# First layer of a graph network: edges sorted by source bucket on the chip and gathered, in place of scatter-adds to DRAM

## The reference

```python
# layer 0: both edge arrays are used with the first row as target
w0_features = x @ w0
w1_features = x @ w1
dst, src = (edge_index[0], edge_index[1])      # edge_index = [src, dst]: the target is the array src
neighbours = segment_sum(w1_features[src], dst, num_segments=N)
x = layernorm(x + relu(w0_features + neighbours))
# layer 1: 8 edge types, 8 heads of 32: GAT with a table per type
h_all = einsum('nf,rof->rno', x, W)
scores = leaky_relu(h_src . attn_src + h_dst . attn_dst)       # per edge and head
w = softmax of scores over the edges of each dst
x = layernorm(x + segment_sum(h_src * w, dst))
```

## Time and profile before

| | us |
|---|---|
| median of 3 runs | 3920.17 (3910.32 to 3921.48) |
| the profiled execution | 3891.99 |
| its span, first to last instruction | 3890.1 |
| POOL busy | 2379.8 (61%) |
| PE busy | 2260.3 (58%) |
| DVE busy | 1898.7 (49%) |
| ACT busy | 1099.7 (28%) |

### The profile page before, as it was taken

One profiled execution on the slowest core, in us unless ns is written; L12 is line 12 of the kernel. 1 busy time (PEld: TensorE's weight loads), 2 busy tenths in 40 slices (PEclk: granted clock), 3 DMA queues, 4 the chain that ended last, 5 costly groups with the idle time before them and its releaser, 6 DMA issues.

```text
span 3890.1 us, 43658 instructions
## 1 busy us (share of the span) xinstructions
PE 2260.3 (58%) x8426; PEld 1550.0 (40%) x8427; DVE 1898.7 (49%) x6684; ACT 1099.7 (28%) x2537; POOL 2379.8 (61%) x1848
## 2 busy tenths in 40 slices
PE   5444444444444444444999926777776676777660
PEld 4333333333333333332555514555545444555440
DVE  2433333333333333332333315777776676777677
ACT  2211222122212221221333303344444333444330
POOL 0477888888888888885111065666666665666601
PEclk8766676666666766676999957888888887888875
DMA  9678876777776767677656433333333333333303
GB/s 339 137 99 136 150 88 88 88 88 88 88 89 88 88 87 88 88 88 165 222 217 227 174 110 82 94 92 98 94 93 93 95 93 89 96 96 96 93 23 114
DMA packets 318535, 443.64 MB, mean 114 GB/s; under 512 B 49188, under 2 KB 273642, under 8 KB 311504
## 3 DMA queue, kind: packets, MB, share of 16 engines
q0 software_dynamic: 169520, 236.24, 38.2%
q1 hardware_dynamic: 141696, 152.01, 13.4%
q10 hardware_dynamic: 7200, 54.07, 3.4%
HBM read 216.80 MB, written 218.81 MB: 112 GB/s over the span
## 4 chain that ended last, share of the span: by engine, by line
issue 31%; PE 29%; DMA 19%; DVE 9%; ACT 5%; POOL 4%; DVEq 1%; another core or an unknown queue 1%; POOLq 0%; ACTq 0%; SPq 0%; PEldq 0%
PE ps L1370 12%; DMA sums_d<-edge_z,idx_slot 11%; PE ps L1315 9%; DMA sums_d<-sums,idx_slot 7%; POOL sums_d L985 4%; PE ps L1361 3%; DVE nodes L636 3%; DVE region L624 2%; ACT edge_z L1083 2%; DVE region L614 1%; PE ps L1223 1%; ACT sums L1083 1%; PE ps L1295 1%; ACT region L1159 1%; DVE region L619 1%
## 5 line engine op out<-in xcount | busy, mean ns | idle before, releaser
L1025 POOL DMA_INDIRECT region<-ha_d,idx_t x880 | 920.5, 1046 | 567.6 <-issue 329.3
L1266 PE MATMUL ps<-region,edge_z 128*128 x1760 | 649.6, 533 | 653.6 <-ACT edge_z L1091 642.4
L1370 PE MATMUL ps<-region 128*128 128x264 f32 x1760 | 681.8, 533 | 375.2 <-DVE nodes L636 236.3
L985 POOL DMA_INDIRECT sums_d<-sums,idx_slot x440 | 689.3, 1567 | 240.6 <-issue 109.6
L985 POOL DMA_INDIRECT sums_d<-edge_z,idx_slot x440 | 686.4, 1560 | 143.9 <-issue 120.1
L1266 PEld LDWEIGHTS ps<-region,edge_z 128*128 128x128 f32 x1760 | 455.2, 272 | 774.9 <-issue 688.4
L1370 PEld LDWEIGHTS ps<-region 128*128 128x128 f32 x1760 | 385.4, 248 | 604.4 <-issue 381.3
L439 DVE TENSOR_TENSOR idx_slot<-dup,edge_z 128x4 int32<-128x4 f32 x220 | 35.9, 163 | 968.8 <-DMA sums_d<-edge_z,idx_slot 512.8
L636 DVE TENSOR_TENSOR nodes<-ps,nodes 128x264 f32 x880 | 378.7, 430 | 141.3 <-DVE nodes L636 68.2
L1315 PE MATMUL ps<-region,edge_z 128*128 128x512 f32 x800 | 351.6, 593 | 0.0
L1361 PEld LDWEIGHTS ps<-edge_z,region 128*128 128x128 f32 x1760 | 276.7, 229 | 80.1 <-issue 62.2
(11 more groups left out here) (173 smaller groups left out, 2567.5 us busy)
## 6 DMA issues: line engine op xcount, KB each, us to landing
ha_d<-region ACTq DMA_DIRECT2D x50, 1056.0 KB, 4.0
row<-step_rows_d SPq DMA_DIRECT2D x220, 128.0 KB
sums_d<-sums SPq DMA_DIRECT2D x4, 6400.0 KB, 28.8
region<-sums_d SPq DMA_DIRECT2D x100, 256.0 KB, 3.7
region<-ha_d,idx_t POOLq DMA_INDIRECT x880
edge_z<-level_d SPq DMA_DIRECT2D x55, 136.0 KB
kl_d<-nodes SPq DMA_DIRECT2D x8, 903.0 KB
edge_z<-kl_d SPq DMA_DIRECT2D x55, 129.0 KB
```

The lines of the kernel that those rows point to most:

```text
L985: g.indirect_dma_start(sums_d[u], bass.IndirectOffsetOnAxis(ap=idx_slot[:, 0, 4 * q + u:4 * q + u + 1], axis=0), sums[h][:, u, :], None, b ...
L1025: g.indirect_dma_start(rows[s][:, k, :], None, ha_rows, bass.IndirectOffsetOnAxis(ap=idx_t[:, B * b + k:B * b + k + 1], axis=0), bounds_ch ...
L1266: mm = t.matmul(ps[:, 2 + 2 * h + u // 2, (u % 2) * D:(u % 2) * D + D], lhsT=counts[h][:, u, :], rhs=y_sb[:, ds(tile[4 * q + u] * D, D)], ...
L1370: t.matmul(ps[:, u, 0:AW], lhsT=sel[q][:, u, :], rhs=rows[s][:, 4 * q + u, :], start=True, stop=True).then_inc(segs, 1)
```

## The change

The scatter loop, `sums_d`, `step_rows_d` and the search for equal sources go. In their place:

1. **Sort.** Edges lie as [128, 896] (row p, column e). The bucket of an edge is `src >> 8`, 25 buckets (BK) of 256 nodes. 13 masks are made on DVE and 12 on ACT, each with its count; TensorE sums the counts over partitions; DVE works out at which column of 128 cells each bucket starts. Then, for each of the 25 buckets, DVE runs a scan over a mask and multiplies it with the bucket's own edges (`put`), and POOL adds the result to `q_row` (128 x 896). The cell numbers are turned by TensorE, and 30 batches (NBT) of 28 columns (TB) move the values to their cells: DVE makes one-hots of 64 places (28 x 64) and three times in four those of 105 windows (28 x 105), ACT the fourth; POOL multiplies the places with the values; TensorE multiplies both (28 matmuls, 64 columns wide) and, after a copy by DVE, by another one-hot of 856 columns from ACT (two matmuls, 428 wide).
2. **Products.** Meanwhile TensorE computes x @ [w1, w0] tile by tile from xT loaded in chunks; y goes to DRAM (`y_d`), x @ w0 to SBUF (`sums0`) as the start of the sums.
3. **Gathered sums.** 856 columns of 128 cells (COLS) in 214 groups of four (NG): POOL gathers 128 rows of `y_d`, ACT makes a one-hot over 256 nodes, TensorE multiplies (two matmuls of 256 columns for each column), DVE adds 128 x 512 into `sums0`. The preparation of the second layer's steps is set between these groups.
4. **Node stage** without `first_product` and without parts: DVE takes the larger of zero and `sums0`, and adds x.

```diff
+            for t in range(BK):
+                if t >= 2:
+                    v.wait_ge(places, t - 1)
+                v.tensor_tensor_scan(count[t % 2], ones[:, 0:1].to_broadcast([P, KR]), masks[t], start[:, t:t + 1],
+                                     ALU.mult, ALU.add).then_inc(scans, 1)
+                if t >= 1:
+                    put(t - 1)
...
+            for t in range(1, BK):
+                g.wait_ge(places, t + 1)
+                g.wait_ge(summed, t)
+                g.tensor_tensor(q_row, q_row, place[t % 3], ALU.add).then_inc(summed, 1)
...
+            for k in range(NBT):
+                places_of(k)
+                if k + 1 < NBT and not on_scalar(k + 1):
+                    windows_of(k + 1)
+                if k:
+                    halves_of(k - 1)
...
+            for k in range(NBT):
+                g.wait_ge(at_made, k + 1)
+                g.tensor_tensor(at[k % 3], at[k % 3], v_col[:, TB * k:TB * k + TB].unsqueeze(2).to_broadcast([P, TB, HC]),
+                                ALU.mult).then_inc(at_filled, 1)
...
+            def move(k):
+                t.wait_ge(at_filled, k + 1)
+                window_ready(t, k)
...
+                for j in range(TB):
+                    mm = t.matmul(ps[0:WW, 2 + k % 2, 0:HC], lhsT=win[k % 4][:, j, :], rhs=at[k % 3][:, j, :],
+                                  start=(j == 0), stop=(j == TB - 1))
+                mm.then_inc(moved, 1)
+            def settle(k):
+                t.wait_ge(halves_made, k + 1)
+                t.wait_ge(s_made, k + 1)
+                for h in range(2):
+                    mm = t.matmul(ps[:, 4 + h, 0:OH], lhsT=halves[k % 2][0:WW, :, :].rearrange("p s n -> p (s n)"),
+                                  rhs=S_c[k % 2][0:WW, h * OH:(h + 1) * OH], start=(k == 0), stop=(k == NBT - 1))
+                mm.then_inc(o_ps, 1)
...
+            def gather_columns(c):
+                if c >= RING:
+                    g.wait_ge(segs0, 4 * (c - RING) + 4)
+                g.sem_inc(pool_turns, 1)
+                for u in range(4):
+                    k = 4 * c + u
+                    g.indirect_dma_start(rows0[c % RING][:, u, :], None, y_d,
+                                         bass.IndirectOffsetOnAxis(ap=y_idx[:, k:k + 1], axis=0),
+                                         bounds_check=node_bound, oob_is_err=True).then_inc(gath[c % 4][c % RING // 4], 16)
...
+            def sum_columns(c):
+                t.wait_ge(gath[c % 4][c % RING // 4], 64 * (c // RING + 1))
+                t.wait_ge(sel0_made, c + 1)
+                for u in range(4):
+                    if c:
+                        t.wait_ge(added0, 4 * (c - 1) + u + 1)
+                    for h in range(2):
+                        mm = t.matmul(ps[:, u, h * D:(h + 1) * D], lhsT=sel0[c % 4][:, u, h * P:(h + 1) * P],
+                                      rhs=rows0[c % RING][:, u, :], start=True, stop=True)
+                    mm.then_inc(segs0, 1)
...
-            def scatter(it):
-                for q in range(4):
-                    h = q % 2
-                    g.wait_ge(sums_copied, 4 * it + q + 3)
-                    g.wait_ge(slots_ready, 4 * it + q + 1)
-                    for u in range(4):
...
-                        g.indirect_dma_start(sums_d[u],
-                                             bass.IndirectOffsetOnAxis(ap=idx_slot[:, 0, 4 * q + u:4 * q + u + 1], axis=0),
-                                             sums[h][:, u, :], None, bounds_check=node_bound, oob_is_err=True,
-                                             compute_op=ALU.add).then_inc(scattered[h][u], 16)
```

More of the change, by code:

```diff
@@ L317, in in_batches, with on_scalar, window_ready @@
                 body(i, i % 4, i // 4)
+        def on_scalar(k):
+            return k % 4 == 0
+        def window_ready(eng, k):
+            if on_scalar(k):
+                eng.wait_ge(win_a, k // 4 + 1)
+            else:
+                eng.wait_ge(win_v, k - k // 4)
+        AT = {"pads": 2, "rows": 12, "firsts": 16, "tiles": 20, "gather": 34, "local": 46, "turn": 50, "edges": 68,
+              "square": 76, "borders": 92, "whole": 108, "links": 124}
         @block.vector
         def _(v):
-            n = [0]
             n = [0]
@@ new lines, in _ @@
+            do(v.tensor_scalar(count[0], bt, float(BK), None, ALU.is_lt))
+            v.scalar_tensor_tensor(out=v_row, in0=v_row, scalar=1.0, in1=count[0], op0=ALU.add,
+                                   op1=ALU.mult).then_inc(v_made, 1)
+            v.wait_ge(v_made, 1)
+            v.wait_ge(sort_ps, PS["counts"])
+            before_p, first_p, past_p, total_p = [ps[:, 7, BK * k:BK * (k + 1)] for k in range(4)]
+            each = ones[:, 0:1].to_broadcast([P, BK])
+            do(v.tensor_scalar(cols_i, total_p, float(P - 1), None, ALU.add))
@@ new lines, in _ @@
+            for g in range(NG):
+                if g % 4 == 0:
+                    some = min(16, COLS - 4 * g)
+                    v.load(bucket_regs[0:some], bucket_row[0:1, 4 * g:4 * g + some])
+                    bucket = [v.snap(r, min_val=0, max_val=BK - 1) for r in bucket_regs[0:some]]
+                add_columns(g, bucket[4 * (g % 4):4 * (g % 4) + 4])
+                if g == AT["pads"]:
+                    pad_rows()
+                if g == AT["rows"]:
+                    edge_rows()
+                if g == AT["tiles"]:
+                    step_tiles()
+                if AT["tiles"] < g <= AT["tiles"] + BLK:
+                    step_tiles_of(g - AT["tiles"] - 1)
+                if g == AT["local"]:
+                    step_places()
+                if AT["turn"] < g <= AT["turn"] + 2 * BLK and (g - AT["turn"]) % 2 == 0:
+                    turned_places((g - AT["turn"]) // 2 - 1)
+                if g == AT["edges"]:
+                    edge_features()
+                if g == AT["square"]:
+                    square_digits()
+                if g == AT["borders"]:
+                    borders()
+                if g == AT["whole"]:
+                    whole_steps()
+                if g == AT["links"]:
+                    link_rows()
+                    SU["end"] = n[0]
@@ L1002, in inverse_deviation @@
+            g.wait_ge(y_ready, 1)
+            for c in range(NG):
+                if 4 * c <= OH < 4 * c + 4:
+                    g.wait_ge(y_ready, 2)
+                gather_columns(c)
+                if c == AT["gather"]:
+                    gather_step_rows()
             def inverse_deviation(it, par):
@@ new lines, in keep_products @@
+            def keep_products(tile):
+                par, h = tile // 2 % 2, tile % 2
+                a.wait_ge(y_ps, tile + 1)
+                if tile >= 4 and h == 0:
+                    a.wait_ge(y_stored[par], 16 * ((tile // 2 - 2) // 2 + 1))
+                a.copy(y_two[par][:, h, :], ps[:, tile % 2, 0:D]).then_inc(y_kept, 1)
+                a.copy(sums0[:, tile * D:(tile + 1) * D], ps[:, tile % 2, D:2 * D]).then_inc(y_done, 1)
+            for tile in range(NT):
+                keep_products(tile)
```

946 lines of the change are left out of this document (510 added, 436 removed).

## The result

The changed kernel takes 3808.57 us (median of 4 runs, 3789.35 to 3825.79), the kernel before 3915.24 in the same comparison (4 runs, 3883.64 to 3921.48): a ratio of 0.9752, 95% interval 0.9714 to 0.9791, so 2.5% faster. I had forecast 3825 us and 2.4%. The profiled execution took 3815.19 us with a span of 3813.4.

The account below looks back on a forecast made before the run. Bound: a 1672 us scatter stage paced by POOL's indirect DMAs. Steps of 45, 130, 18, 414, 1154 and 398 us start the second layer at 2163 instead of 2258 us; own time 3797 plus 28 gives 3825 us, range 3665 to 3910.

Parts of the forecast that it names:

- Step 1: Start to the counts: edges and bucket numbers by 15 us, then masks and small operations; 45 us.
- Step 2: Bucket loop: VectorE's scan and multiply and GpSimd's add exclude each other, 5.1 us a bucket; 130 us.
- Step 4: The 30 batches of moves: TensorE mostly at 1.2 GHz, 13.8 us a batch; 414 us.
- rival (a): Moves: TensorE gets 2.4 GHz, VectorE with GpSimd sets 9.0 us a batch; 144 us less, 3681 us; chance 0.22.
- Step 5: Gather stage: GpSimd's issue paces it, 1.33 us a gather, 5.3 us a group, the rest fits under; 1154 us.
- theory C: Gather stage, from the experiments' expectations: TensorE's clock sets the stage; separate semaphores would bring no change.
- rival (c): Gather stage: TensorE stays at 1.2 GHz, 7.5 us a group, 1605 us, total 4282 us; chance 0.10.
- Step 6: Node stage: 10 us to the first table, then 25 pairs at 15.05 us; 398 us.
- the 28 us I added: Total: the earlier kernel's profiled execution was 28 us below its runs' median, so 28 us were added to 3797.

Follow-up runs that it names:

- early_masks: Changed kernel with VectorE making the masks before the small tensors that wait for attention loads, and 17 masks in place of 13; 3791.88 us, ratio 0.972.
- no_fill: Changed kernel without GpSimd's multiply in the moves, so all gathered rows are wrong or row 0; 4018.7 us, ratio 1.028, moves 214 us.
- together: Changed kernel with 17 VectorE masks, VectorE's own fill, and eight banks with one news increment per four columns from column 288; 3748.57 us, ratio 0.9605.
- one_gather: Changed kernel with three of the four gathers of each group left out; 3363.44 us, ratio 0.8645, gather stage 847 us.
- no_adds: Changed kernel without VectorE's first-layer adds and TensorE's wait for them; 3756.94 us, ratio 0.9656, gather stage 1240 us.

## Why the prediction was right, and where it was not

**Step 1, to the counts, was 17 us short.** The arithmetic of the masks held (2.1 us each, twelve in 25 us), but not their start: I had let VectorE have the bucket numbers at 15 us, with 28 as the far bound. It had them at 28.8, after waiting for the attention loads until 25.0; the edges landed no earlier, as early_masks shows. Two small readings were off as well: the two prices that I took from the earlier trace rows give 1.0 ns for each further element, not 0.83 (a pass over 896 took 1.04 us, forecast 0.95, with less wait between), and the 64 short passes, which the earlier trace rows price at 0.20 us and I at 0.17, took 13.8 us in place of 11, hidden behind the masks.

**Step 2, the bucket loop, held**: 124.4 us for 25, 5.0 each. The scan takes 2.03 us (forecast 1.9), the multiply 1.06, GpSimd's add 2.07. The exclusion I read from the earlier trace rows is plainer here, in two pieces in order of time of the changed kernel:

```profile
90.48 4.00 DVE L462 TENSOR_TENSOR_SCAN region<-ones,region 128x896 f32<-128x896 f32 x1
90.52 2.07 POOL L1087 TENSOR_TENSOR region<-region 128x896 f32<-128x896 f32 x1 [2.94 <-DVE region L456]
```

The scan's record begins 0.04 us ahead of the add's, but it took 4.00 us, while the first two scans, beside which GpSimd did nothing, took 4.06 together. So the scan did its work after the add. The Trainium skill (SBUF — State Buffer, section "SBUF: two separate sides") says that two such instructions exclude each other for the whole of one, and by that rule the trace agrees.

**Step 4, the moves, failed by its share of half clock.** I had put 13.8 us a batch, nine of ten at 1.2 GHz, and it was 8.4 on average, most at 2.4 GHz. The prices at either level were nearly right and a little high: 12.8 us at half clock (forecast 14.3), and with the exclusion 6.7 to 8.1 (forecast 9.0). The fast level itself was a little better than I had it: 6.6 us a batch for TensorE alone (forecast 7.9). I had reasoned from the earlier trace rows that so few dense columns would leave TensorE slow, and had read there that the clock, once it fell among the 16-column passes, stayed at 0.50. It did not stay. In the kernel before it was low for 10.2 us, and this line of the same view follows:

```profile
98.00:118.00 20.00, 13.76 (x56) 1.00 0.95 361
```

In no_fill, where it never waits, it was at full clock from the third batch to the last. So rival (a), to which I gave 0.22, is what happened in this stage. Its price was set by the exclusion, as it said: VectorE's first operation took 2.02 us when alone and up to 5.01 beside the fill, the fill 3.19 alone and 6.10 in the median. Taking the fill away from GpSimd gave 36 to 40 us (together, no_fill) against this execution's 254, and 25 at the least against the shortest of the eleven, 243. The Trainium skill (TensorE: Matmul & The Clock Gate, section "Part 1: The HAM clock gate") says that activity of the engine releases the throttle; by its rule the moves should have been fast, and they were. A dip of 10 us was too thin a row to rest 414 us on.

**Step 5, the gathers, failed by what it left out.** Each of its prices holds: a gather took 1.012 us, with 0.3 between them 1.317 where nothing else was late, an add 0.69 and 0.21, a column of passes 0.86 us at full clock. None of them is the bound. What failed is that I took what must fit under GpSimd's issue at its price alone: beside four gathers a group the news of TensorE's results, or its passes, came late, and a group took 6.1 us where I had 5.3. The clock is a small part of it: with four gathers 137 of 856 columns ran at half clock, in one_gather 19, and 118 columns at 0.85 us more are 100 us (an estimate), of 430 between the two stages. So theory C, the clock alone, is too small. The runs shown exclude as causes the bytes, the rows, GpSimd's being busy, the number of banks, the number of increments, who waits on a semaphore, and VectorE's adds. They leave the gather instruction itself, issued four times a group. Which part of it does the harm, whether the harm grows with their number, and on which path it reaches TensorE is not shown: the increments come late while VectorE answers at once, and in no_adds the passes themselves come in steps of 0.70 us, but no run here tells passes that are held up from increments that are.

In size this is what rival (c) feared: I had written that it decides from 5.8 us a group, the point at which the whole saving of 95 us is gone, and the stage went past that. The mechanism was another, since the clock was 0.84 and not 0.50, and the kernel was still faster only because the moves had given back 164 us.

**Step 6 held.** A pair takes 15.07 us (1790.98 to 1806.05 in the chain), forecast 15.05. The 18 us more between the last gather and the first table have another source: VectorE's last add ended 28 us after the last gather's issue, where I had allowed 6. GpSimd is not the bound and runs ahead by its ring of eight groups. In one_gather, without late news, it was 32 us.

**The second layer**, not changed, took 1650.6 us in this execution, 18 more than before. In the fourteen executions profiled, all with this part unchanged, it took 1618 to 1651 us, the kernel before's 1632 among them, so this is scatter and not an effect. The same holds for the 28 us I added to come from one execution to the median: the changed kernel's profiled one was 7 us above its median.

The forecast that the kernel gets 2.4% faster was thus met with the sign and the size right, but the size by luck: two of its six terms were wrong by 164 and 134 us in opposite directions. With the moves as forecast and the gathers as measured the kernel would have been slower than before. A row of the kernel before might have made me look, and I had not weighed it. In its view of waits, TensorE's weight loads in the second layer, beside the gathers there, wait for nothing that the profile names:

```profile
PEld ps L1370 <- issue: 381.3, 316, 6.5
```

Whether that is the same effect was not tried. Late increments are not seen there: of the 609 recorded for these passes (of 880), 593 stand within 0.3 us of a pass's end.

## What to carry to other kernels

Before counting on a stage of indirect DMAs to be paced by their issue, measure it beside the TensorE work that it feeds: here a group took 6.1 us beside four gathers, where no engine's own work was over 5.3, whatever the gathers moved, and no room in banks brought it back. Work that VectorE and GpSimd hand to each other with SBUF operands on both sides is priced as a sum; giving GpSimd's share to VectorE made the moves 36 us shorter than in the changed kernel's profiled execution. And a forecast whose largest terms hang on the clock needs both levels carried to the end for each stage, because the short waits that one engine imposes decide it.

## What the hardware showed that I had not expected

- TensorE's passes or their increments came late beside GpSimd's gather instructions: 6.1 us a group of sums with four, 4.1 (VectorE's own work) with one, the same with 128 bytes a row as with 1 KB and with 64 rows as with 128; plain loads of the same size and a busy GpSimd did nothing. The Trainium skill (SBUF — State Buffer, section "Who interferes with whom") says that DMA never contends with a compute engine and that TensorE and ScalarE never wait on anyone. That section is about SBUF's ports, and no run here shows that a port is the cause; but whoever reads it as a promise that TensorE keeps its pace beside gathers is corrected by these runs.
- Gathers that all read one row of DRAM kept the DMA engines busy for 0.88 of the time at 81 GB/s (no_fill); gathers of spread rows needed 0.39 for 105 GB/s.
- It was the increment of TensorE's semaphore that came late and not VectorE's answer: in the changed kernel 441 of 728 recorded increments stand within 0.3 us of the end of a column's last pass, with one gather a group all 849; of VectorE's 304 late adds, 240 began within 0.2 us of a recorded increment.
- TensorE kept 2.4 GHz through 28 batches of 64-column passes in which it never waited (no_fill), and fell to 1.2 GHz, for 10.2 or 34.1 us at a time, in the changed kernel, where it had waited for GpSimd by 0.6 to 1.5 us in most batches (7.2 or 8.1 us from batch to batch in place of 6.6). In together, with 7.2 us in every fourth batch, it did not fall.
